# Feed-forward products from float16 parts in a four-stage transformer kernel

## What is computed

```python
x = x + attn_a(ln(x))   # 16 heads of 64, biases, softmax over all keys, + ln(x), layer norm, gamma, beta
x = x + ffn(ln(x))      # h = relu(v @ W1 + b1);  h @ W2 + b2;   W1 128x512, W2 512x128
x = x + attn_b(ln(x))   # 8 heads of 128, rotary, causal
x = x + ffn(ln(x))      # the same W1, b1, W2, b2
```

## Time and profile before

| | us |
|---|---|
| median of 3 runs | 1936.58 (1933.06 to 1937.72) |
| profiled execution | 1935.38 |
| its span in the trace | 1933.6 |

### The profile page before, as it was taken

How to read it: one execution, slowest core, us unless ns; L and a number is a source line. 1 busy time by engine, 2 the same in 40 slices (tenths; PEclk the granted TensorE clock), 3 DMA queues, 4 the chain that set the end, 5 groups by cost and what they waited for, 6 DMA issues and landing times.

```text
span 1933.6 us, 55434 instructions
## 1 busy us (share of the span) xinstructions
PE 1865.8 (96%) x23343; PEld 1267.0 (66%) x23343; DVE 1420.6 (73%) x2613; ACT 1546.5 (80%) x1919; POOL 1598.4 (83%) x1025
## 2 busy tenths in 40 slices
PE   4899999999999999999999999779999999999998
PEld 3566666666666666666666666547777777767766
DVE  7788778778777878877877875566767767767652
ACT  4799999999998898898898899646666666666664
POOL 3899999999999999999999999358787787887752
PEclk8999999999999999999999999889999999999999
DMA  6101101100100100100100100100000000000000
GB/s 147 35 11 26 34 14 23 35 15 21 35 18 19 34 19 18 35 18 18 35 18 18 35 2 2 55 1 2 2 1 2 2 2 1 2 1 2 2 2 23
DMA packets 45032, 37.94 MB, mean 20 GB/s; under 512 B 8304, under 2 KB 44144, under 8 KB 44528
## 3 DMA queue, kind: packets, MB, share of 16 engines
q1 hardware_dynamic: 44304, 34.00, 7.5%
q10 hardware_dynamic: 480, 0.39, 0.1%
HBM read 8.15 MB, written 1.05 MB: 5 GB/s over the span
## 4 chain that ended last, share of the span: by engine, by line
PE 81%; POOL 8%; issue 5%; DVE 4%; ACT 1%; DMA 0%; ACTq 0%; POOLq 0%; DVEq 0%
PE ST L1594 11%; PE ST L1595 11%; PE RING L1479 7%; PE OO L1560 6%; PE OO L1562 6%; POOL PBUF L695 6%; PE OO L1559 6%; PE OO L1479 4%; PE ST L1787 2%; PE ST L1794 2%; PE ST L1793 2%; PE ST L1792 2%; PE ST L1659 2%; PE OO L1680 1%; PE RING L1572 1%
## 5 line engine op out<-in xcount | busy, mean ns | idle before, releaser
L611 POOL TENSOR_TENSOR PAB<-PR,PAB 128x1024 f16<-128x1024 f32 x342 | 724.1, 2132 | 48.3 <-ACT PAB L787 47.6
L787 ACT ACTIVATE PAB<-ST,exp_scale 128x1024 f16<-128x1024 f32 x512 | 567.5, 1108 | 0.0
L1089 DVE TENSOR_REDUCE maxes<-RING 128x1 f32<-128x512 f32 x661 | 440.3, 685 | 132.1 <-PE RING L1479 127.7
L1559 PE MATMUL OO<-VP,PAB 128*128 128x66 f16 x4096 | 446.7, 192 | 2.4 <-POOL PAB L611 2.4
L1560 PE MATMUL OO<-VP,PAB 128*128 128x64 f16 x4096 | 447.2, 193 | 0.0
L1562 PE MATMUL OO<-VP,PAB 128*128 128x66 f16 x4096 | 445.2, 192 | 0.0
L785 ACT ACTIVATE PR<-ST,exp_scale 128x1024 f32<-128x1024 f32 x342 | 381.7, 1116 | 73.4 <-PE ST L1595 70.7
L1559 PEld LDWEIGHTS OO<-VP,PAB 128*128 128x128 f16 x4096 | 380.5, 96 | 77.3 <-issue 15.4
L1560 PEld LDWEIGHTS OO<-VP,PAB 128*128 128x128 f16 x4096 | 377.1, 97 | 61.3
L1594 PE MATMUL ST<-QL,KH 128*128 128x512 f16 x1024 | 388.6, 379 | 1.9 <-DVE QH L1101 1.0
L1595 PE MATMUL ST<-QH,KL 128*128 128x512 f16 x1024 | 388.8, 380 | 0.0
(11 more groups left out here) (305 smaller groups left out, 3962.0 us busy)
## 6 DMA issues: line engine op xcount, KB each, us to landing
KH<-HS SPq DMA_DIRECT2D x124, 64.0 KB, 2.0
QL<-HS SPq DMA_DIRECT2D x64, 64.0 KB, 2.0
QL<-LS SPq DMA_DIRECT2D x64, 64.0 KB, 2.1
QH<-HS SPq DMA_DIRECT2D x64, 64.0 KB, 2.0
KL<-LS SPq DMA_DIRECT2D x62, 64.0 KB, 2.0
X<-in_L_attn_a_x SPq DMA_DIRECT2D x4, 256.0 KB, 3.8
SHARED<-in_rope_cos SPq DMA_DIRECT2D x1, 1024.0 KB, 4.9
SHARED<-in_rope_sin SPq DMA_DIRECT2D x1, 1024.0 KB, 7.0
```

Of the source, the lines that this page charges most:

```text
L611: pool.tensor_tensor(PB[:, s, :], PRA[g % PR_SLOTS], PA[:, s, :], ALU.subtract).then_inc(p_low_ready, 1)
L787: act.activation(PA[:, step % SLOTS_A, :], ST[step % 2][:, :], ACT.Exp, scale=scale).then_inc(sa.exps, 1)
L1089: dve.reduce_max(maxes[:, i // BLOCKS, i % BLOCKS:i % BLOCKS + 1], bank[:, :], X_AXIS).then_inc(sa.ring_taken, 1)
L1559: pe.matmul(o, high, v[:, 0:V2_AT], start=(m == 0 and qt == 0), stop=False, skip_group_check=True)
```

## The change

W1 with b1, and W2, get a power-of-two scale each, taken with the scales of the second attention's weights: ACT squares them, DVE sums them (`sum_squares_fw`), and the tables `b_sums` to `b_down` grow by two columns. W1 and b1 lie in one tile `W1B1` now, scaled in place (`scale_fw`). The product of the two back scales is `fw_back`, applied in `take_ffn`. W1 and W2 are split into `W1H`, `W1L`, `W2H`, `W2L` inside the attentions.

The second product is three float16 products for each float32 one, in both rounds. For that `relu` writes float32 into one buffer `HIDF` (in `PAB`), DVE casts a quarter into the high half of `HID[b % 2]` (`high_hidden`), and POOL writes the difference into the low half (`low_hidden`). The first product is three float16 products in the last round only, and the turned blocks there are split into `XH` and `XL`. The last two blocks are turned into two banks (`TURN_LAST`), the first of them ahead of the first `ffn_out`, the other right behind it.

```diff
@@ POOL
+            def low_hidden(r, b):
+                for j in range(CH):
+                    n = (r * BLOCKS + b) * CH + j
+                    pool.wait_ge(hid_high, n + 1)
+                    pool.tensor_tensor(HID[b % 2][:, 1, j, :], HIDF[:, j, :], HID[b % 2][:, 0, j, :], ALU.subtract
+                                       ).then_inc(hid_low, 1)
@@ ACT, set-up
+            act.wait_ge(fw_in, 48)
+            act.activation(fw_squares[:, 0, :], W1B1[:, :], ACT.Square, scale=float(np.sqrt(D))).then_inc(b_squared, 1)
+            act.activation(fw_squares[:, 1, 0:CH * D], W2s[:, :, :].rearrange("p j c -> p (j c)"), ACT.Square,
+                           scale=float(np.sqrt(D))).then_inc(b_squared, 1)
@@ ACT, first attention
+                if (u, step) == (5, 0):
+                    act.wait_ge(b_scaled, 1)
+                    act.activation(W2H[:, :, :], W2s[:, :, :], ACT.Copy, scale=b_up[:, FW2:FW2 + 1]).then_inc(fw_high, 1)
@@ ACT, relu
-                wait(act, ffn_put, r * BLOCKS + b - 1)
-                act.activation(HID[b % 2][:, j, :], QUARTER[j], ACT.Relu, bias=b1c[:, j:j + 1]
-                               ).then_inc(hid_ready, 1)
+                wait(act, hid_low, n - CH + 1)
+                act.activation(HIDF[:, j, :], QUARTER[j], ACT.Relu, bias=b1c[:, j:j + 1]).then_inc(hid_full, 1)
@@ ACT, last blocks
-                act.activation(XNT[:, b * BLK:(b + 1) * BLK], O[0][:, :], ACT.Copy).then_inc(xnt_ready, 1)
+                act.activation(XH[:, b * BLK:(b + 1) * BLK], TURN_LAST[b - 2][:, :], ACT.Copy).then_inc(xh_ready, 1)
@@ DVE
+            def scale_fw():
+                dve.wait_ge(b_scaled, 1)
+                dve.tensor_tensor(fw_back[:, :], b_down[:, FW1:FW1 + 1], b_down[:, FW2:FW2 + 1], ALU.mult)
+                dve.tensor_scalar(W1B1[:, :], W1B1[:, :], b_up[:, FW1:FW1 + 1], None, ALU.mult).then_inc(fw_scaled, 1)
+            def split_w2():
+                dve.wait_ge(fw_high, 1)
+                dve.scalar_tensor_tensor(W2L[:, :, :], W2s[:, :, :], b_up[:, FW2:FW2 + 1], W2H[:, :, :], ALU.mult,
+                                         ALU.subtract).then_inc(fw_low, 1)
...
+                if u == 2 and step in (3, 4):
+                    sum_squares_fw(step - 3)
+                if (u, step) == (4, 4):
+                    scale_fw()
+                if (u, step) == (5, 4):
+                    split_w2()
...
+            def high_hidden(r, b, j):
+                n = (r * BLOCKS + b) * CH + j
+                dve.wait_ge(hid_full, n + 1)
+                wait(dve, ffn_put, r * BLOCKS + b - 1)
+                dve.tensor_copy(HID[b % 2][:, 0, j, :], HIDF[:, j, :]).then_inc(hid_high, 1)
...
-                dve.tensor_tensor(a, a, O[1][:, :].rearrange("p (a c) -> p a c", c=D), ALU.add
-                                  ).then_inc(x_ready, 1)
+                dve.scalar_tensor_tensor(a, O[1][:, :], fw_back[:, 0:1], a, ALU.mult, ALU.add).then_inc(x_ready, 1)
...
-                dve.tensor_copy(XNT[:, b * BLK:(b + 1) * BLK], bank[:, :]).then_inc(sbb.ring_taken, 1)
+                link(dve.tensor_copy(XH[:, q], bank[:, :]))
+                dve.tensor_tensor(XL[:, q], bank[:, :], XH[:, q], ALU.subtract).then_inc(sbb.ring_taken, 1)
@@ PE
+                    pe.matmul(QUARTER[j], W1H[:, part], XH[:, q], start=True, stop=False)
+                    pe.matmul(QUARTER[j], W1L[:, part], XH[:, q], start=False, stop=False)
+                    pe.matmul(QUARTER[j], W1H[:, part], XL[:, q], start=False, stop=True).then_inc(hid_put, 1)
...
-                pe.wait_ge(hid_ready, (r * BLOCKS + b + 1) * CH)
+                pe.wait_ge(hid_low, (r * BLOCKS + b + 1) * CH)
                 for i in range(BT):
...
-                        ins = pe.matmul(O[1][:, i * D:(i + 1) * D], HID[b % 2][:, j, i * P:(i + 1) * P],
-                                        W2s[:, j, :], start=(j == 0), stop=(j == CH - 1))
+                        pe.matmul(o, high, W2H[:, j, :], start=(j == 0), stop=False)
+                        pe.matmul(o, high, W2L[:, j, :], start=False, stop=False)
+                        ins = pe.matmul(o, low, W2H[:, j, :], start=False, stop=(j == CH - 1))
```

More of the change, by code:

```diff
@@ L705, in _ @@
                     low_b((head + 1) % 2, j, (head + 1) * 2 * BLOCKS + j, F[:, j % 2, :])
-            for b in range(BLOCKS):
-                add_b2(1, b)
+            add_b2(1, 0)
+            add_b2(1, 1)
+            low_hidden(1, 0)
+            add_b2(1, 2)
+            low_hidden(1, 1)
+            add_b2(1, 3)
+            low_hidden(1, 2)
+            low_hidden(1, 3)
         @block.scalar
@@ L902, in _ @@
                         values_high_b(1 - hs, item[1], RING3B[n % 3], n)
+                if (it, ul, step) == (0, 6, 1):
+                    act.wait_ge(fw_scaled, 1)
+                    act.activation(W1H[:, :], W1s, ACT.Copy).then_inc(fw_high, 1)
                 if head + 2 < HB and (qb, step) == (2, 10):
@@ L1323, in _ @@
             settle_ffn(0)
+            for j in range(CH):
+                high_hidden(0, 2, j)
             settle_ffn(1)
+            for j in range(CH):
+                high_hidden(0, 3, j)
             low_block(BLOCKS + 1, 0, TURN_B[0])
@@ L1361, in _ @@
                 place = g - (len(PLACES_B) - TILES)
+                if (it, ul, step) == (0, 6, 4):
+                    split_w1()
                 if place == 1:
@@ L1398, in _ @@
             take_output(sbb, RING3B[(n + 1) % 3], n + 1, X, BLOCKS - 1)
+            for j in range(2):
+                high_hidden(1, 0, j)
             dve.wait_ge(sbb.ring_taken, n + 2)
             last_ln(3)
+            for j in range(2, CH):
+                high_hidden(1, 0, j)
             normalise(4 * BLOCKS + 3, 3)
-            for b in range(BLOCKS):
+            for j in range(CH):
+                high_hidden(1, 1, j)
+            low_block(2 * BLOCKS + 1, 2, TURN_LAST[0])
+            take_ffn(1, 0)
+            low_block(2 * BLOCKS + 2, 3, TURN_LAST[1])
+            for j in range(CH):
+                high_hidden(1, 2, j)
+            take_ffn(1, 1)
+            for j in range(CH):
+                high_hidden(1, 3, j)
+            for b in range(2, BLOCKS):
                 take_ffn(1, b)
@@ L1894, in _ @@
                 hidden_part(1, 1, j)
+            pe.wait_ge(xn_ready, 3 * BLOCKS + 3)
+            turn_block(3 * BLOCKS + 2, 2, TURN_LAST[0])
             ffn_out(1, 0)
-            for b in range(2, BLOCKS):
-                pe.wait_ge(xn_ready, 3 * BLOCKS + b + 1)
-                wait(pe, xnt_ready, 3 * BLOCKS + b - 2)
-                turn_block(3 * BLOCKS + b, b, O[0])
-                hidden(1, b)
-                ffn_out(1, b - 1)
+            pe.wait_ge(xn_ready, 3 * BLOCKS + 4)
+            turn_block(3 * BLOCKS + 3, 3, TURN_LAST[1])
+            hidden(1, 2)
+            ffn_out(1, 1)
+            hidden(1, 3)
+            ffn_out(1, 2)
             ffn_out(1, 3)
```

86 lines of the change are left out of this document (63 added, 23 removed).

## The result

The changed kernel takes 1944.09 us, the median of 8 runs (1940.9 to 1946.74). The kernel before, on the same chip, takes 1935.72 (8 runs, 1932.17 to 1938.18). The ratio is 1.0043, with an interval of 1.0033 to 1.0052: slower by 0.4%, 8.4 us. The prediction was 1944.0.

The account below looks back on a forecast made before the run. TensorE bounds the kernel before; after, the relay of ScalarE, VectorE and GpSimd bounds both feed-forwards. +5.2 (first feed-forward) +1.4 (last) +2.0 (attentions) = +8.6 us on 1935.38 gives 1944.0 us, range 1930 to 1951, likeliest case 1940 to 1948.

Parts of the forecast that it names:

- What TensorE gains: Both feed-forwards: float16 products save 0.91 us in each of 8 blocks and 0.86 in each of 4, 10.7 us on TensorE alone.
- Casts and differences exclude each other: Both feed-forwards: VectorE's SBUF casts and GpSimd's differences cannot run together, add up to 7.1 us a block and become the bound.
- Rival A: Both feed-forwards: casts run beside GpSimd, differences follow at 1.12 us, -1.3 and -4.1 us, 1930.5 us in all; chance 0.2.
- The pace: Both feed-forwards: each difference of 1.12 us plus a cast of 0.34 us, one after the other.
- +5.2 us: First feed-forward: term for the relay of ScalarE, VectorE and GpSimd with its delays; -1.3 us without exclusion.
- The end: Last feed-forward: last difference at 1927.8, end at 1931.4, so +1.4 us; -4.1 us without exclusion.
- the chaining of before: Last feed-forward: the kernel before, chained with the same durations, ends at 1930.1; base of the +1.4 us.
- Rival B: Both feed-forwards: TensorE's idle spells drop its clock to half once in each, +5 us, so 1949 us; chance 0.15.
- Settling behind the casts: First feed-forward: sum and statistics of the last x block start about 1233.9 instead of 1226.42, part of +5.2 us.
- Inside the attentions: Both attentions: added sums, scalings and splits of the weights cost +2.0 us, bounds 0 to 6.
- the scaling: First attention: VectorE's scaling of W1 and b1, 516 elements by a pointer scalar, takes 0.67 us.
- the price of the earlier trace: Attentions: 2.1 us lost by VectorE cost TensorE 0.92 us, so 0.44 us per us.

Follow-up runs that it names:

- Version 7: Changed kernel without GpSimd's 32 differences; the third product of each chunk reads the high part again, casts stay: 1925.74 us, ratio 0.9951.
- version 3: Changed kernel, but VectorE makes the high float16 part from the PSUM bank instead of casting ScalarE's float32 tile in SBUF: 1935.42 us, ratio 1.0002.
- version 4: Changed kernel, but ScalarE makes the high part with a second relu from PSUM and VectorE casts nothing: 1932.62 us (0.9991), again 1936.20 (0.9992).
- version 8: version 4 with GpSimd's first differences ahead of bias sums and the last block's second product in float32: 1933.57 us, ratio 0.9982.
- version 6: Changed kernel with the settling (sum and statistics) of the last block moved back ahead of the first four casts: 1939.89 us, ratio 1.0017.
- version 1: Changed kernel with both feed-forwards put back into float32, keeping only the weights' work inside the attentions: 1938.46 us, ratio 1.0009.
- versions 2: version 1 with the last feed-forward as in the changed kernel (float16 parts, two banks), the first still float32: 1939.10 us, ratio 1.0018.

## Why the prediction was right, and where it was not

**What TensorE gains (10.7 us): right.** Version 7 shows 11.1 in the two feed-forwards, 2.8 and 8.3 for the predicted 3.6 and 7.1. In the first, TensorE waits 1.6 us for ScalarE's copy of a turned block, a wait that the kernel before does not have there. The second has 1.4 us from elsewhere: before, TensorE waited that long for ScalarE's copies of the turned blocks, and with two banks it does not. Without it, 6.9 stand against 7.1.

**Casts and differences exclude each other: right, and shown.** The shortest cast is 0.41 us, predicted 0.42; TensorE waits before its second products for GpSimd; version 3 takes the exclusion away from casts and differences and changes no order, and gets 7 to 9 us back. Rival A is the kernel in which this does not happen, 1930.5; it is out, because the differences stand at 1.24 to 1.37 us each while casts run and not at 1.12. Versions 3 and 4, where casts and differences do not meet, show its two terms: -1.3 predicted for the first feed-forward, 0.0 measured (-1.3 with the order of version 8); -4.1 for the end, -2.0 and -4.6 measured.

**The pace was too dark.** Differences and casts do not add up to 1.46 us; four differences take 4.97 to 5.49 us, 1.24 to 1.37 each. In a block with casts a difference is 0.14 to 0.17 us longer in the median than without (1.30 and 1.33 for 1.16), half of the 0.34 that the prediction added. It is one reason why the first feed-forward is +3.8 and not +5.2 us; the term that was sized wrong is the standing of GpSimd for a cast.

**The end: +1.1 for +1.4, by luck in part.** The last difference ended at 1931.04 in a run whose second attention ended 4.3 us later than before; taken back by that, 1926.7, against 1927.8 predicted. So GpSimd was 1.1 us better than priced. The clock took 1.8 us: half clock in most of the last product, 4.4 us for 2.66. And the chaining of before, from which the +1.4 is counted, ends at 1930.1, where the trace has its last sum end at 1930.85: 0.75 us too early. The three nearly cancel (-1.1 + 1.8 - 0.75). Rival B had this mechanism, for both stretches and at 5 us. In the first feed-forward it did not come: the granted clock is 0.99 and 1.00 from 1230 to 1260, and 0.84 from 1260 to 1270 as before (0.83). In version 4 the last product runs at full clock, from 1923.38 to the sum at 1926.33, 2.9 us.

**Settling behind the casts: right in kind, too small in size.** The prediction has the sum start at 1233.9 and block 1's relus 4.6 us later. It started at 1234.73, took 1.57 us for 0.74, and is 2.9 of the 3.8 us (version 6).

**Inside the attentions: +2.0 predicted; +0.5 by the two profiled runs, +1.9 by version 1's median.** The step that failed is the scaling, taken as 0.67 us, at the pace of an operation from PSUM and free of GpSimd, for which the prediction names no row. It took 2.44. The same form at the end, VectorE's normalisation of the last block, shows it with four pieces at once (timeline): alone, then beside differences. Version 7, without differences, has 1.11 us at both places; version 4, with differences and without casts, 4.35 us at the second.

```profile
1902.85 1.11 DVE L998 TENSOR_SCALAR XN<-X,meanvar,rstd 128x128 f32<-128x128 f32 x4
...
1908.28 3.57 DVE L998 TENSOR_SCALAR XN<-X,meanvar,rstd 128x128 f32<-128x128 f32 x4
```

The end of the prediction's chain did not have these 2.5 us either. The Trainium skill, page "SBUF — State Buffer", section "Who interferes with whom", names tensor_scalar among the operations that can take the shared ports; the rows agree. It does not hold for every operation of VectorE with one input from SBUF: the statistics (L985, one tensor in, one out) take 0.23 to 0.30 us in all 80 cases of the changed kernel, beside differences too (four in 0.87 us at 1245.18). By the price of the earlier trace rows, 0.44 us of TensorE for one of VectorE, the other 1.77 us are 0.8 us; moving the operation gave 3.2 by the medians. The rest of that gain stays open.

**The total.** 1944.0 stands against 1944.1. The forecast added its 8.6 us to the profiled execution of before (1935.38), not to the median of the three runs it had (1936.58, which would give 1945.2); the median of eight is 1935.72. With its own median as the base the forecast would have been 1.1 us high. The terms were too high in the first feed-forward (1.4 us) and at the end (0.3), and the profiled difference of 5.5 us is smaller than 8.6 for that reason and for the second attention's -1.5. The medians differ by 8.4 because the profiled run is the fastest of its eight. What the other seven have more of lies, as far as one can tell from version 4's two profiles, in the attentions: the same program took 1226.6 and 610.5 us there in one profiled run and 1228.5 and 613.4 in another, on another chip (1931.64 and 1936.34 us in all), with 59.1 and 59.0, 30.1 and 30.1 in the feed-forwards. The forecast's accuracy to 0.1 us is chance; its three terms were each off by up to 1.5 us.

## What to carry to other kernels

When a step is taken off TensorE and given to VectorE and GpSimd in turns, price the pair of them together: a cast or a scaling by a pointer scalar that VectorE makes from SBUF into SBUF and an operation of GpSimd did not run side by side here, and the same result made from PSUM, or by ScalarE, was free of that, even where the instruction itself is slower (0.74 us for 0.41; 1.0002 and 0.9991 of the time before for 1.0043). Look also at what stands behind a waiting cast in VectorE's queue: one moved settling step was worth 2.9 us.

## What the runs showed of the hardware that was not expected

- A float32 tensor_scalar with pointer scalars, SBUF to SBUF, waits for GpSimd's operations: four pieces of 128 take 1.11 us alone, 3.57 and 4.35 us beside them, and one of 516 elements takes 2.44 us. The statistics of a layer norm, also from SBUF to SBUF with one input, do not wait (0.23 to 0.30 us).
- Under full load the exclusion costs GpSimd less than the cast's own time: 1.16 us a difference alone, 1.30 to 1.33 with casts between, so 0.14 to 0.17 for a cast of 0.41.
- TensorE's clock fell to half in the last 9 us after it had been waiting between bursts (busy 6.63 of 10 us in the slice before), and the final product took 1.8 us longer; the mean clock of 0.81 is the same in versions 2 and 6.
- Two profiled executions of one program, on two chips, differ by 4.7 us in 1932, all of it in the two attentions; a single profile doesn't price an edit of 2 us there, though it does in the feed-forwards, which repeat to 0.1 us.
